# Weight loads and the router's store on ScalarE's DMA queue, and V's and K's steps at other slots, in an attention kernel with a router

## The reference, cut to what matters

```python
# x: 4 batches x 512 tokens x 512
xn = _layernorm(x)
# attention, 16 heads of 128 (q, k, v per head), linear, with a decay s per head
q, k, v = split(silu(xn @ w_qkv.T))
for block in blocks:                      # along the 512 tokens
    o_inter = (q * exp(-s * i)) @ kv
    o_intra = ((q @ k.T) * exp(-s * (i - j))[i >= j]) @ v
    kv = exp(-s * BLK) * kv + (k * exp(-s * (BLK - j))).T @ v
out = norm_w * out * rsqrt(mean(out * out, all heads) + EPS)
s = (sigmoid(xn @ w_gate.T) * out) @ w_out.T
# router: softmax over 64 experts, the best 8
g = silu(xn * sum(top_w) + top_w @ expert_bias[top_idx])
return x + s * g
```

## Time and profile before

| | before |
|---|---|
| median of 3 runs (lowest to highest) | 1124.48 us (1121.88 to 1125.41) |
| the profiled execution: time, span | 1128.39 us, 1126.6 us |
| mean granted TensorE clock | 0.987 |
| TensorE busy | 1064.7 us (95%), 5540 matmuls |
| ScalarE, VectorE, GpSimd busy | 627.1, 663.0, 648.7 us |
| moved by DMA | 141.92 MB, 126 GB/s, 39.4% of the 16 engines' time |

### The profile page before, as it was taken

How to read it: one execution, slowest core, us unless ns; L and a number is a source line. 1 busy time by engine, 2 the same in 40 slices (tenths; PEclk the granted TensorE clock), 3 DMA queues, 4 the chain that set the end, 5 groups by cost and what they waited for, 6 DMA issues and landing times.

```text
span 1126.6 us, 15056 instructions
## 1 busy us (share of the span) xinstructions
PE 1064.7 (95%) x5540; PEld 896.9 (80%) x5540; DVE 663.0 (59%) x1093; ACT 627.1 (56%) x1118; POOL 648.7 (58%) x636
## 2 busy tenths in 40 slices
PE   7799999989999999999979989999999989999997
PEld 6587887878778787887868878888877878878885
DVE  6256556565666677676535655645656565555557
ACT  6467556555555556565544545656555465555543
POOL 5757555555555647556545873655556464655613
PEclk9899999999999999999989989999999999999999
DMA  3233332242533544544654652323334352332335
GB/s 132 98 119 107 94 94 94 89 162 87 168 120 110 159 127 149 169 129 143 248 181 128 194 171 77 109 90 103 99 112 141 99 168 85 99 107 70 104 111 194
DMA packets 128490, 141.92 MB, mean 126 GB/s; under 512 B 40352, under 2 KB 95776, under 8 KB 128416
## 3 DMA queue, kind: packets, MB, share of 16 engines
q1 hardware_dynamic: 128416, 140.95, 39.4%
HBM read 95.83 MB, written 45.09 MB: 125 GB/s over the span
## 4 chain that ended last, share of the span: by engine, by line
PE 69%; DMA 10%; DVE 9%; ACT 9%; issue 2%; POOL 1%; SPq 0%; DVEq 0%; ACTq 0%
PE BS L170 6%; PE BS L172 6%; PE BS L171 6%; PE PX L170 5%; PE PX L172 5%; PE PX L171 5%; DMA dkt<-P 5%; PE BA L170 4%; PE BA L172 4%; PE BA L171 4%; PE PO L726 4%; PE BD L170 4%; PE PS L642 3%; PE BD L172 3%; PE BD L171 3%; PE PT L691 3%
## 5 line engine op out<-in xcount | busy, mean ns | idle before, releaser
L480 POOL TENSOR_TENSOR WL<-ST,WH 128x768 fp32r<-128x768 f32 (+1 forms) x128 | 165.0, 1292 | 172.2 <-ACT WH L476 172.1
L480 POOL TENSOR_TENSOR WL<-STG,WH 128x512 fp32r<-128x512 f32 (+1 forms) x128 | 129.7, 1014 | 150.2 <-ACT WH L476 150.1
L170 PE MATMUL BS<-XH,WH 128*128 128x512 f32 x384 | 162.4, 423 | 13.1 <-ACT K L565 12.7
L172 PE MATMUL BS<-XH,WL 128*128 128x512 f32 x384 | 152.6, 397 | 0.0
L171 PE MATMUL BS<-XL,WH 128*128 128x512 f32 x384 | 151.8, 395 | 0.0
L791 DVE TENSOR_TENSOR Y<-Y,PX 128x512 f32<-128x512 f32 x104 | 71.2, 685 | 103.8 <-PE PX L172 103.3
L770 DVE TENSOR_TENSOR GL<-G,GH 128x512 fp32r<-128x512 f32 x64 | 74.3, 1162 | 77.6 <-ACT GH L766 77.6
L749 POOL TENSOR_TENSOR SS<-SS,SQ 128x512 f32<-128x512 f32 x60 | 92.0, 1533 | 43.6 <-ACT SQ L741 43.6
L170 PE MATMUL BA<-XH,WH 128*128 128x512 f32 x256 | 106.8, 417 | 6.4 <-ACT VT L600 5.7
L170 PE MATMUL BD<-XH,WH 128*128 128x512 f32 x256 | 107.2, 419 | 3.8 <-DVE K L556 2.7
L649 DVE TENSOR_TENSOR P<-PS,DQ 128x512 f32<-128x512 f32 x64 | 44.2, 691 | 110.1 <-ACT KD L680 96.2
(11 more groups left out here) (298 smaller groups left out, 2494.1 us busy)
## 6 DMA issues: line engine op xcount, KB each, us to landing
STG<-in_wp SPq DMA_DIRECT2D x80, 512.0 KB, 3.5
dvt<-VB SPq DMA_DIRECT2D x64, 256.0 KB, 2.0
VB<-dvt SPq DMA_DIRECT2D x64, 256.0 KB, 2.8
dkt<-P SPq DMA_DIRECT2D x60, 192.0 KB, 1.9
P<-dkt SPq DMA_DIRECT2D x60, 192.0 KB, 2.6
XR<-in_x SPq DMA_DIRECT2D x38, 256.0 KB, 3.1
dgd<-XR SPq DMA_DIRECT2D x16, 256.0 KB, 3.5
dxh<-WT SPq DMA_DIRECT2D x8, 448.0 KB, 3.3
```

The lines of the kernel that those rows point to most:

```text
L170: eng.matmul(o, ah, bh, start=first, stop=False, skip_group_check=skip)
L172: return eng.matmul(o, al, bh, start=False, stop=last, skip_group_check=skip)
L480: a = op("pool", lambda e, dst=dst, src=src: e.tensor_tensor(WL[:, u, dst], src, f32(WH[:, u, dst]), ALU.subtract))
```

## The change

`dma` gets an argument for the issuing engine. `w_load` issues on ScalarE (the first three loads stay on SyncE) and is no longer called by `w_parts` and `o_parts` but planned at slots of its own, three slots behind the step that read the buffer; the wait for GpSimd's reading goes with it to ScalarE. The store of `g_make` is issued by ScalarE too, behind the Silu that makes its data. The transposes of V and K stay on SyncE, and their reads back (`v_back`, `k_back`) are put ahead of the other steps of their slot. V's copy comes five or six slots behind its turn instead of four. K's scaling comes one slot later. Scores come three slots later, two behind the scaling. All steps of batch 1 from `states` on come a slot later. The last cycle keeps its slots for the heads, but not for V.

```diff
-        def dma(s, f):
+        def dma(s, f, e="sp"):
...
-            prog["sp"].append(lambda eng: f(eng).then_inc(s, 16))
+            prog[e].append(lambda eng: f(eng).then_inc(s, 16))
...
-        def w_load(n):
+        def w_load(n, e="act"):
             c, k = divmod(n, 5)
-            wait("sp", *(stg_free[n % 3] or ()))
+            wait(e, *(stg_free[n % 3] or ()))
             tk["stg", n] = dma(s_stg[n % 3], lambda e: e.dma_start(
-                STG[:, n % 3, :], wp[c % NPAIR, kind(4 * c + k) if k < 4 else k]))
+                STG[:, n % 3, :], wp[c % NPAIR, kind(4 * c + k) if k < 4 else k]), e)
...
                 if i == 3:
                     stg_free[n % 3] = (a,)
-                    if n + 3 < 5 * CYC:
-                        w_load(n + 3)
...
             stg_free[n % 3] = (a,)
-            if n + 3 < 5 * CYC:
-                w_load(n + 3)
...
             a = op("act", lambda e: e.activation(dst, dst, ACT.Silu))
-            wait("sp", a)
+            wait("act", a)
             xr_free[kg] = tk["gd", h, b, t] = dma(s_gs[kg], lambda e: e.dma_start(
-                dgd[2 * h + b, t * 128:(t + 1) * 128, :], dst))
+                dgd[2 * h + b, t * 128:(t + 1) * 128, :], dst), "act")
...
         def v_steps(c, base):
-            o = int(c < CYC - 1)
-            for s, r, b in ((4, 0, 0), (9, 0, 1), (16 + o, 1, 0), (21 + o, 1, 1)):
+            for s, e, r, b in (((4, 9, 0, 0), (10, 15, 0, 1), (17, 22, 1, 0), (23, 28, 1, 1)) if c < CYC - 1 else
+                               ((4, 9, 0, 0), (9, 14, 0, 1), (15, 20, 1, 0), (20, 25, 1, 1))):
                 plan(base + s, v_turn, c, r, b)
-                plan(base + s + 1, v_back, c, r, b)
-                plan(base + s + 4, v_copy, c, r, b)
+                at.setdefault(base + s + 1, []).insert(0, (v_back, (c, r, b)))
+                plan(base + e, v_copy, c, r, b)
...
-                for b, o in ((0, (3, 4, 7, 7, 9, 11, 13, 13, 14, 15)), (1, (8, 9, 12, 12, 13, 15, 17, 17, 18, 19))):
+                for b, o in ((0, (3, 4, 8, 10, 9, 11, 13, 13, 14, 15)), (1, (8, 9, 13, 15, 14, 16, 18, 18, 19, 20))):
                     for f, k in zip(steps, o):
-                        plan(s + k, f, c, r, b)
+                        if f is k_back:
+                            at.setdefault(s + k, []).insert(0, (f, (c, r, b)))
+                        else:
+                            plan(s + k, f, c, r, b)
...
+        plan(3, w_load, 3)
+        plan(6, w_load, 4)
         for c in range(CYC):
             b0 = SLOTS * c
             plan(b0 + (27 if c + 1 < CYC else 18), o_parts, c)
+            if c + 1 < CYC:
+                plan(b0 + 30, w_load, 5 * c + 7)
...
                     plan(s + 7 - (k == 0), w_parts, g + 2, (2, 3))
+                    n = 5 * ((g + 2) // 4) + (g + 2) % 4 + 3
+                    if n < 5 * CYC:
+                        plan(s + 10 - (k == 0), w_load, n)
...
         for n in range(3):
-            w_load(n)
+            w_load(n, "sp")
```

## The result

The changed kernel takes 1132.33 us (median of 7 runs, 1129.06 to 1137.98) against 1124.48 (1121.88 to 1126.39, 7 runs beside it): a ratio of 1.0074, 95% interval 1.0048 to 1.0101. It is slower by 0.7%, clear of the interval, where 1099 was forecast. The profiled execution takes 1130.59 us with a span of 1128.8 and a mean granted clock of 0.982 (before 0.987).

What follows compares the result with a forecast made beforehand. TensorE, busy 1064.7 of 1126.6 us, was taken as the bound; only its gaps and lower-clock time could be saved. Terms summed to -25.2 us: 1128.4 to 1103.2 profiled, 1099 off the median, range 1084 to 1118.

Steps and rivals of the forecast that it cites:

- router mixture: Four stretches where TensorE loses 3.5 us each, 14 us, to waits behind `g_make`'s Silu; expected 2.4 us saved in all.
- The store: `g_make`'s store, issued by ScalarE behind the Silu's end: 0.4 us each time; upper bound counted four at 0.55 per stretch.
- `gate_low`: Batch 1's step moved from slot 26 to 27, behind VectorE's K addition that frees bank BD: -2.1 us, bounds 0 and -2.7.
- rival C: More is gained: earlier `g_make` removes most of the 14 us and the new waits, 1086 us off the median; chance 0.14.
- moves taken at nothing: K's read back behind V's wait at slots 10, 11, and `keep_u2` at slots 22, 36: 0 us, bounds 0 and +8.
- cycle ends: V's copy and two evictions ahead of KD delay `states`: 0.5 us at six ends, +3.0, bounds 0 and +22.
- KD through SyncE's queue: Batch 1's K no longer behind two weight loads: six waits gone, -10.7 us, bounds -4 and -10.7; their clock -4.3.
- the second half's 4.4: Longest KD wait, while transformed X is read back at 550 to 575 us: left at 4.4 us, bounds -3 and +2.
- First V: Slots 8 to 9: `keep_u2` ahead of V's copy cuts TensorE's 4.60 us wait by 3.8; clock at 50 to 75 us, -2.8.
- Decays: Batch 1's KD follows six exponentials; `states` waits about 2.4 us instead of 0.86 and 1.07: 0, bounds -2 and +2.
- VectorE's wait for KD: VectorE's 96.2 us in 42 waits before the product of scores; expected nearly gone in the trace after.
- Rival A: Slower: slot 30's weight load lands too late for ScalarE's copy at slot 32; 1141 us at 9 us landing; chance 0.08.

Runs made afterwards that it cites:

- steps alone: Changed kernel's moved slots of V, K, scores and batch 1, with every DMA on SyncE and loads called where they were before: 1113.67 us, ratio 0.9903.
- V's old slots: Changed kernel with head 1's V back at its earlier slots (turns 17 and 22, copies 21 and 26): 1122.51 us, ratio 0.9979.
- the three repairs: Changed kernel with the router's store on SyncE, `gate_low` of head 0, batch 1 at slot 28, and head 1's V at its old slots: 1099.72 us, ratio 0.9774.
- slot 28: Changed kernel with `gate_low` of head 0, batch 1 at slot 28 instead of 27: 1118.00 us, ratio 0.9950.

## Why the prediction was wrong

The step that failed first is the **router mixture**, put at -2.4 us with bounds -10 and +9. Its four cycles became 10.4 us longer. Two parts were mis-sized.

*The store* was priced at 0.4 us of issue, hidden because `evict` is no later than before. It measured 9 to 10.5 us in all (steps alone with and without it; kernel after with and without it). The price is ScalarE's standing still from the issue's wait for the Silu, some 0.5 us at each of 16, in the stretch where that engine is late anyway; with twelve of the 16 freed, 6 of the 11 us in the router cycles came back. The upper bound of 0.55 a store was the value to take.

*`gate_low`* was looked at for the addition that it makes room for (right: the waits of 1.67 and 1.06 us became 0.43 and none), not for what stands behind it at its new slot. There the normalization takes 2.59 us, TensorE waits 2.24 four times, and with the clock 10.6 to 14.3 us hang on it. That the order at slot 27 is the cause is shown. That the 2.59 us come from GpSimd's operation is seen in its end, and no run took GpSimd away altogether: in the kernel before, 13 of the 20 normalizations of this form took 0.90 us or more, and each of the 13 ended 0.27 to 0.29 us behind a GpSimd operation that ran beside it; the other seven took 0.50 to 0.54. In the kernel after, the four of 2.59 ended 0.28 us behind GpSimd's pass.

By the Trainium skill ("SBUF — State Buffer", section "SBUF: two separate sides") VectorE and GpSimd share a pair of ports that is locked for a whole instruction, by a GpSimd operation or by a VectorE operation in a two-port mode or with two inputs in SBUF; whichever starts first holds it, and the other blocks. The ends agree with it; in which mode the normalization runs, no run shows.

With both put right, and V's old slots, the four cycles take 261.6 us, 13.4 less than before, where -2.4 was forecast; that is close to the 14 us of rival C, whether by its reason is not shown. So it is chance that the three repairs end at the forecast's 1099.

The second step that failed is the **moves taken at nothing**, with the second queue beside them. That V's wait holds K up costs one wait of 0.7 us at most in the steps alone. But the weight load that ScalarE now issues just ahead of V's write makes V's trip 2.0 us longer at the median, and K's write stands behind it. The prediction had estimated 1.7 us for what a load on the second queue does to K, and left it out of its sum. This is where the six **cycle ends** went: forecast at 0.5 us each, 3.0 in all, they are 2.35 and 2.43 in cycles 4 and 6 and 0.26 to 0.70 in the other four, 6.8 in all; in the steps alone one of 0.73 is left of the six, with the weights on ScalarE and the store on SyncE they are 7.9, and with V's old slots 1.5. V's old slots are worth 9.8 us in all.

**KD through SyncE's queue** came in size: the six waits for the second K of a cycle, 10.7 us before, are 3.4 now (2.21 became 1.10, 3.77 became 2.29, four are gone). The path to it was only half right. The steps alone, with the loads still ahead of K on SyncE, have 5.0 in these six, and of the 9.0 us that cycles 7 and 8 win they win 7.2. At the worst place K's write still goes out 4.3 us after its transposition, before 4.8, since a load of x ahead of it waits on SyncE, and its trip takes 6.03 us where it took 5.94 (645.27 to 651.30, 643.28 to 649.22):

```profile
654.46 0.94 PE L687 MATMUL PT<-V,KD 128*128 128x128 f32 x6 [2.29 <-ACT KD L676]
```

Three other kernels with the weights on ScalarE (the store on SyncE, slot 28, V's old slots) wait 3.66 to 4.49 there, so the 2.29 is in part luck. The clock in 650 to 675 went from 0.86 to 1.0, and the second half's 4.4 is 2.8.

Below all of them lies the sum itself: it treated the two halves of the change as one gain. The queue (weights) takes the loads from ahead of K; the later slots make K's lateness harmless. Either does most of it alone: outside the router cycles the queue wins 13 us with the old slots, and the weights on it lose 10 there with the new ones (8.2 of the median). In cycles 4 to 6 it is 11.1 us (205.5 against 194.4): V's order with the load beside it is 3.7 of them by the kernel with V's old slots; cycle 5 stays 3.1 us longer with all repairs (69.3 against 66.2), and there ScalarE waits 8.8 us for dxl where the steps alone have 5.2. That this last is the DMA engines' sharing is argued from the landing times only. No run moved the load of slot 24 alone, away from V's write: it is the test that is missing.

**First V** was right (4.60 became 0.40), its clock was not: TensorE now waits 3.03 us at 57.19 for VectorE's K addition, which the router's parts hold up, so 50 to 75 us stays at 0.86 and the start gains 2.0 instead of 6.6.

```profile
47.02 0.50 PE L170 MATMUL BS<-XH,WH 128*128 128x512 f32 x1 [0.40 <-ACT K L561]
...
57.19 0.80 PE L170 MATMUL BD<-XH,WH 128*128 128x512 f32 x1 [3.03 <-DVE K L552]
```

**Decays**: 2.40 and 2.42 as forecast, but with the clock 2.3 us dearer, not 0. **VectorE's wait for KD** fell from 96.2 to 4.8. **Rival A** named the late load of slot 30: it was late (6.5 us near 233 us), ScalarE waiting 3.00, 0.18, 2.89 and 3.44 us in the four router cycles and not every cycle, and the store was why.

## What to carry to other kernels

Before a DMA is given to an engine that computes, look at what it waits for: an issue that waits for that engine's own last result stops the engine until the result is out, here some 0.5 us each time. Look also at what the other queue issues at that moment: here a 512 KB load 0.2 us ahead of a 256 KB write made that tile's trip 4.4 us instead of 2.0 to 2.4. When two edits cure the same lateness, price each on top of the other, and list what stands behind a moved step on each engine at its new place, not only what it leaves. Time each part alone and in pairs: the kernel that is slower by 0.7% held one that is faster by 2.3%.

## What the hardware showed that was not expected

- A normalization on VectorE of 0.5 us took 0.90, 1.09, 2.07 or 2.59 us, as it met GpSimd's operations, and ended 0.27 to 0.30 us behind them.
- A weight load on ScalarE's queue 0.2 us ahead of V's write on SyncE's made V's trip 4.4 us at the median instead of 2.4; 0.8 to 1.7 us behind it, it left the trip at 2.0 to 2.6.
- With two issuers the weight loads landed in 3.8 us instead of 3.5 and dxl in 6.1 instead of 4.5 (4.3 in the steps alone).
- The clock can decide as much as the gaps: with `gate_low` at slot 28 idle time of 3 us less went with 14.3 us less time, in the steps alone 7 us less with 10.6. A wait of 2.4 us was followed by 0.93 in the window at 100 us in the kernel after and in the steps alone, but not in the kernel with slot 28, whose waits there are the same.
